# Small work beside the steps of two mixture-of-experts stages, cut into more pieces and placed at other steps

## The chip, the cores and the metric

The kernel runs on one core of a Trainium2 chip. A core has a matrix engine (TensorE, PE in the profile; its weight loads are PEld), a vector engine (VectorE, DVE), an activation engine (ScalarE, ACT), a general engine (GpSimd, POOL) and a queue that issues transfers (SyncE, SP). Each runs its own instruction list strictly in order, and they meet through semaphores. The metric is the device time of one execution in microseconds (us), lower is better; the median of three runs is given.

## The reference

The input is 2048 tokens of width 128. Four layers each hold an attention block and a feed-forward block, all in the same sandwich:

```python
x = x + _layernorm(_L2_ffn_ref(_layernorm(x, axis=-1), ...), axis=-1)   # 16 experts, top 4 of 2 groups, and a shared one
x = x + _layernorm(_L3_attn_ref(_layernorm(x, axis=-1), ...), axis=-1)  # linear attention
x = x + _layernorm(_L3_ffn_ref(_layernorm(x, axis=-1), ...), axis=-1)   # 8 experts, top 2
```

Only these last three of the eight blocks matter here. The first of them multiplies silu(gate) by up and takes it through down, for every expert and token, weighted by the routing. The attention takes q and k through elu(.) + 1, makes one product of keys and values over the 1024 tokens of a sequence (two chunks of the kernel), multiplies q by it and projects. The last block is softmax routing, gelu between two matrices per expert, and a weighted sum.

## The kernel before

Its stages are numbered by block: stage 5 is the 16-expert mixture, stage 6 the linear attention, stage 7 the 8-expert mixture. A stage handles the tokens in four chunks of 512 (c = 0 to 3), a chunk is four tiles of 128. Stage 5 has 25 steps per chunk (r), each one slice of hidden units; stage 7 has 32 (m). Stage 6 has no stretch of its own: it runs in pieces beside the steps of 5 and 7, as do the routing and everything between the blocks.

**A step of stage 5.** TensorE makes gate and up (three matmuls each, L1762 to L1764, since every operand is split into a rounded part and a rest) and, for the step three earlier, down (L1768, L1769, L1771; L1771 reads the rest). ScalarE makes silu of the gate (L1863), then copies the upper part of the last product (L1851). VectorE multiplies the gate by its weight (L1909), makes the rest of the last product (L1899) and then the product of gate and up (L1917). Down results gather in one bank, which ScalarE evicts (L1855) in step 2 of the next chunk.

**A step of stage 7.** TensorE: three matmuls for the hidden units, three for the step four earlier. ScalarE: gelu (L2174), copy (L2180), every fourth step an eviction. VectorE: the rest (L2249) and one of four stations of the weighted sum (L2225 to L2241). Its loops may be five steps apart at most (a ring of five buffers).

**Small work.** Functions named beside (pe_, act_ and dve_beside_moe5 and _moe7) say after which step of its main loop each engine does which small piece. Each engine counts its own steps, and an engine may be several steps ahead of another, so a piece in step 9 of TensorE and one in step 9 of VectorE don't run at the same time. The pieces:

- dve_y: statistics of a block's result (STY, MVY); GpSimd makes the scale of them. dve_x: adds the scaled result to the stream (L282), then makes statistics of the sum (L264, L267 into MVX). GpSimd (pool_x, L333 to L338) then normalises the rows into XN, pe_turn_x turns them (L397), act_turned copies them.
- lin_features, in part 0 and part 1 for each chunk: TensorE, ScalarE (exponential and relu, L1482 to L1494, with a table load before and one back to silu behind) and VectorE (L1502, L1507). lin_kv is TensorE's product of keys and values (L1514), which reads the features of two chunks; then lin_out and lin_proj.
- dve_route5_a to _d and dve_route7_a to _c: routing. In stage 7 ScalarE makes an exponential between a and b and one between b and c (L2060). turn_weights then turns the routing's weights (L2065), which a transfer spreads over the partitions later.

## Time and profile before

| | |
|---|---|
| median of 3 runs | 1632.12 us (1631.22 to 1632.94) |
| the profiled execution | 1629.69 us, its span 1627.9 us |
| TensorE's mean granted clock | 0.877 of full speed |
| busy over the span | PE 79%, DVE 66%, ACT 70%, POOL 17% |
| stage 5 | 1108 to 1382 us of the span |
| stage 7 | 1382 to 1628 us |

The profile is one execution. Its busy shares are means over eight blocks with different limits (the first two thirds are attention, where ScalarE's line L1035 alone is busy for 466 us), so the stretches of the two mixture stages are read apart. In a row, the number in square brackets at the end is how long the engine had been idle before the instruction, and what ended the idle time. Matmuls overlap, so a row's own duration is longer than the distance to the next.

### The profile page before, as it was taken

The numbers are of one execution on the slowest core, as the hardware profiler recorded it, in microseconds if no ns is written. First come the engines' busy times: TensorE is split into PE (matmuls) and PEld (weight loads), VectorE is DVE, ScalarE is ACT, GpSimd is POOL, SyncE is SP. The second block draws the span as 40 slices with busy tenths as digits, with TensorE's granted clock in tenths as the row PEclk, the third lists the DMA queues.
The fourth block names the chain that finished last, engine by engine and source line by source line (L and its number), as shares of the span: only waits on it lengthen the run. The fifth ranks groups of instructions, "written<-read, shape, count | busy, mean of one in ns | idle before, by whom it ended". The sixth has DMA issues, their size and how long they took to land.

```text
span 1627.9 us, 22138 instructions
## 1 busy us (share of the span) xinstructions
PE 1288.8 (79%) x8028; PEld 659.5 (41%) x8028; DVE 1079.5 (66%) x2031; ACT 1140.7 (70%) x1619; POOL 271.1 (17%) x361
## 2 busy tenths in 40 slices
PE   5598888876676777777777777678988988887996
PEld 2233333344011111111111144456767776665875
DVE  6877877054455664566456655556978679767898
ACT  3166777755999999999999834345555645876985
POOL 4500003042000000000000034083011034803000
PEclk9589999997688788878877899888999998999998
DMA  5611020002410000101000030002323225011111
GB/s 178 154 22 22 23 41 3 2 1 87 107 20 0 20 17 4 20 0 20 20 1 1 1 151 1 1 1 66 106 83 93 88 73 171 27 33 33 47 44 54
DMA packets 40765, 74.65 MB, mean 46 GB/s; under 512 B 6096, under 2 KB 10448, under 8 KB 39888
## 3 DMA queue, kind: packets, MB, share of 16 engines
q1 hardware_dynamic: 39792, 71.67, 15.6%
q10 hardware_dynamic: 864, 1.57, 0.3%
q8 instruction: 63, 1.03, 0.3%
q14 instruction: 46, 0.38, 0.1%
HBM read 59.26 MB, written 13.96 MB: 45 GB/s over the span
## 4 chain that ended last, share of the span: by engine, by line
PE 38%; ACT 24%; DVE 19%; issue 12%; POOL 4%; DMA 2%; SPq 0%; POOLq 0%; DVEq 0%; ACTq 0%
ACT SHARED L1035 15%; PE PS L823 4%; PE PS L992 4%; PE PS L979 3%; DVE NM L732 3%; DVE SHARED L1045 3%; PE PS L712 2%; PE PS L645 2%; PE PS L1762 2%; PE PS L787 2%; PE PS L1764 2%; PE PS L1763 2%; DVE KS L1917 2%; PE PS L1215 2%; PE PS L1771 2%
## 5 line engine op out<-in xcount | busy, mean ns | idle before, releaser
L1035 ACT ACTIVATE SHARED<-PS 128x1536 f32<-128x1536 f32 (+1 forms) x352 | 466.1, 1437 | 31.2 <-PE PS L979 30.2
L979 PE MATMUL PS<-QS,KS 51*128 51x512 bf16 (+1 forms) x1024 | 242.0, 461 | 134.1 <-ACT SHARED L1035 128.7
L1045 DVE TENSOR_TENSOR SHARED<-SHARED 128x1536 f32<-128x1536 f32 (+1 forms) x176 | 286.6, 1703 | 86.4 <-ACT SHARED L1035 86.4
L803 ACT ACTIVATE SHARED<-PS 128x512 f32<-128x512 f32 (+3 forms) x384 | 164.4, 494 | 96.6 <-PE PS L791 87.3
L979 PEld LDWEIGHTS PS<-QS,KS 51*128 51x128 bf16 (+1 forms) x1024 | 41.2, 99 | 386.8 <-ACT SHARED L1035 358.6
L992 PE MATMUL PS<-SHARED,Vg 128*16 128x512 f32 x1024 | 157.9, 694 | 1.7 <-DVE SHARED L1045 1.6
L732 DVE TENSOR_REDUCE NM<-PS 128x2 f32<-128x1024 f32 (+3 forms) x128 | 129.0, 1022 | 28.5 <-PE PS L718 20.4
L1762 PE MATMUL PS<-ROUNDED 128*128 128x512 f32 x328 | 138.8, 423 | 4.9 <-ACT KS L1863 4.2
L1763 PE MATMUL PS<-ROUNDED 128*128 128x512 f32 x328 | 132.5, 404 | 0.0
L1764 PE MATMUL PS<-ROUNDED 128*128 128x512 f32 x328 | 132.3, 403 | 0.0
L1851 ACT ACTIVATE ROUNDED<-KS 128x512 fp32r<-128x512 f32 x100 | 63.0, 630 | 82.8 <-DVE KS L1917 82.8
L1771 PE MATMUL PS<-ROUNDED 128*128 128x512 f32 x228 | 94.1, 413 | 22.3 <-DVE ROUNDED L2249 11.4
L476 POOL COPY Vg<-XH 128x256 f32<-128x256 f32 x16 | 6.3, 400 | 626.9 <-PE PS L992 396.9
L326 POOL TENSOR_SCALAR VEY<-MVY 128x4 f32<-128x4 f32 x32 | 8.4, 263 | 583.8 <-DVE MVY L267 582.6
L823 PE MATMUL PS<-SHARED,Vg 128*16 128x256 f32 (+3 forms) x1152 | 93.3, 397 | 11.2 <-ACT SHARED L803 9.6
L1768 PE MATMUL PS<-ROUNDED 128*128 128x512 f32 x228 | 92.1, 404 | 8.3 <-ACT ROUNDED L2180 3.7
L2249 DVE TENSOR_TENSOR ROUNDED<-KS,ROUNDED 128x512 fp32r<-128x512 f32 x103 | 75.1, 732 | 30.5 <-ACT ROUNDED L2180 29.7
L712 PE MATMUL PS<-SHARED 48*128 48x512 bf16 (+3 forms) x384 | 71.2, 370 | 29.9 <-DVE NM L732 18.4
L1769 PE MATMUL PS<-ROUNDED 128*128 128x512 f32 x228 | 91.2, 400 | 0.0
L2174 ACT ACTIVATE KS<-PS,C 128x512 f32<-128x512 f32 x103 | 71.1, 691 | 27.3 <-PE PS L1764 26.0
L1863 ACT ACTIVATE KS<-PS 128x512 f32<-128x512 f32 x100 | 58.8, 588 | 40.1 <-PE PS L1764 39.9
L1909 DVE TENSOR_TENSOR SHARED<-KS,SHARED 128x512 f32<-128x512 f32 x88 | 61.4, 698 | 35.3 <-ACT KS L1863 32.2
(265 smaller groups left out, 2314.4 us busy)
## 6 DMA issues: line engine op xcount, KB each, us to landing
SHARED<-wx SPq DMA_DIRECT2D x64, 256.0 KB, 3.1
qx<-SHARED SPq DMA_DIRECT2D x24, 256.0 KB, 4.0
SHARED<-in_moe SPq DMA_DIRECT2D x3, 1600.0 KB, 11.9
kx<-SHARED SPq DMA_DIRECT2D x18, 256.0 KB, 4.0
SHARED<-wx SPq DMA_DIRECT2D x16, 224.0 KB, 3.0
SHARED<-qx SPq DMA_DIRECT2D x16, 192.0 KB, 4.7
SHARED<-kx SPq DMA_DIRECT2D x16, 192.0 KB, 5.3
QS<-qx SPq DMA_DIRECT2D x16, 192.0 KB, 4.5
```

What stands on the lines that cost most here:

```text
L712: ins = pe.matmul(PS[:, slot(k, x):slot(k, x) + n], q[r, p, qt * P:qt * P + P], key[r, p, hi * CH:hi * CH + n], start=True, stop=not diag)
L732: dve.tensor_reduce(out=dst, in_=src, axis=AX.X, op=ALU.max, negate=True).then_inc(A[0, "a_red"], 1)
L803: act.activation(PB[t % 3][:, h, q0:CH], bank(RING0[n % 3], q0), ACT.Exp, scale=SCORE_SCALE)\
L823: ins = pe.matmul(PS[32 * h:32 * h + VC, 6 * CH + a:6 * CH + b], Vg[g % 2][:, kt, h, :], PB[t % 3][:, h, a:b], start=kt == 0, stop=last an ...
L979: ins = pe.matmul(bank((v % 2) * GRP + f - a), KS[g % 2][r, h // 2, kt * P:kt * P + P], QS[g % 2][r, h // 2, qh * CH:(qh + 1) * CH], start ...
L992: ins = pe.matmul(PS[32 * h:32 * h + VC, 6 * CH:7 * CH], Vg[g % 2][:, kt, h, :], EX[:, f * CH:f * CH + CH], start=kt == 0, stop=kt == KT - 1)
L1035: act.activation(dst, PS[:, (v % 2) * GRP * CH:((v % 2) * GRP + b - a) * CH], ACT.Exp if second == qh else ACT.Sigmoid, scale=SCORE_SCALE)\
L1045: dve.tensor_tensor(ex_tile(j), ex_tile(j), GR[w % RING][:, 0:(b - a) * CH], ALU.mult)\
L1762: pe.matmul(dst, w[0], x[0], start=start, stop=False)
L1763: pe.matmul(dst, w[0], x[1], start=False, stop=False)
L1764: return pe.matmul(dst, w[1], x[0], start=False, stop=stop)
L1771: return pe.matmul(dst, w[0], x[1], start=False, stop=stop)
```

## The change

The arithmetic stays. dve_x is cut in two, dve_x_sum (the addition) and dve_x_stats (the statistics), which may stand in different steps. Routing pieces are cut: b and c of stage 5 into b, b2 and c, c2; b of stage 7 into b and b2 (dve_top_k gives its second half to dve_top_k_ties). The two y pieces ahead of stage 7 get a step each. Where both halves are called in a row, nothing changes. The rest of the change is step numbers in the six tables:

| piece | before | after |
|---|---|---|
| stage 5, c 0: routing, VectorE | 4, 8, 12, 16 | 4, 7, 10, 13, 16, 19 |
| turned weights, TensorE / ScalarE | 20 / 21 | 22 / 23 |
| c 1, 2: x, VectorE | 6 | sum 7, statistics 8 |
| turning of x, TensorE / ScalarE | 9 / 10 | 11 / 12 |
| features part 0, TensorE / ScalarE / VectorE | 11 / 12 / 13 | 13 / 14 / 15 |
| features part 1, the same | 15 / 16 / 16 | 16 / 17 / 18 |
| c 2: kv, TensorE / VectorE | 18 / 18 | 19 / 20 |
| out, TensorE / ScalarE; proj | 20 / 21; 23 | 21 / 22; 24 |
| c 2, 3: y of the first two chunks for stage 7 | c 2: 24, 24 | c 3: 0, 1 |
| c 3: their x, VectorE | 0, 1 | sum 2, 3; statistics 3, 4 |
| their turning, TensorE / ScalarE | 4, 5 / 5, 6 | 6, 8 / 7, 8 |
| logits, TensorE; VectorE | 7, 8; 8 | 9, 10; 11 |
| y and x of chunk 2 for the attention, VectorE | 10, 12 | 13; sum 15, statistics 16 |
| its turning, TensorE / ScalarE | 17 / 18 | 19 / 20 |
| routing a, b, (b2,) c, VectorE | 9, 11, 13 | 12, 14, 17, 18 |
| its exponentials, ScalarE | 10, 12 | 13, 17 |
| turned weights, TensorE / ScalarE | 16 / 17 | 21 / 22 |
| stage 7, c 0: features (2, part 1), TensorE / ScalarE / VectorE | 9 / 10 / 11 | 8 / 9 / 11 |
| other attention pieces of c 0 | 10 to 27 | one step later; proj stays at 31 |
| c 1: y, y, VectorE | 1, 1 | 1, 2 |
| x, x, VectorE | 3, 5 | sum 4, 6; statistics 5, 7 |
| turnings, TensorE / ScalarE | 9, 10 / 10, 11 | 11, 13 / 12, 14 |
| logits, TensorE / VectorE | 14, 14 / 15, 15 | 16, 17 / 17, 18 |
| routing a, b, (b2,) c, VectorE | 16, 19, 24 | 19, 22, 24, 28 |
| its exponentials, ScalarE | 17, 22 | 20, 26 |
| turned weights, TensorE / ScalarE | 28 / 29 | 30 / 31 |
| c 2, 3: last x and shift, VectorE | 18, 22 | sum 18, 22; statistics and shift 19, 23 |

The lines of the diff that are more than a number, and of the numbers those of which the text speaks most:

```diff
@@ dve_x @@
         def dve_x(dve, own, e, c):
+            dve_x_sum(dve, own, e, c)
+            dve_x_stats(dve, own, e, c)
+
+        def dve_x_sum(dve, own, e, c):
             if e.norm_y:
...
                 ins.then_inc(x_sum, 1)
-                dve.wait_ge(x_sum, e.n_y(c))
...
+        def dve_x_stats(dve, own, e, c):
+            if e.norm_y:
+                dve.wait_ge(x_sum, e.n_y(c))
             if e.turn:
                 dve_stats(dve, own, STX, MVX, lambda t: tile(e.stream(), t), c).then_inc(x_var, 1)
...
-            own.link(dve.tensor_reduce(out=best[:, :, 7:8], in_=sel, axis=AX.X, op=ALU.add))
+            own.mark(dve.tensor_reduce(out=best[:, :, 7:8], in_=sel, axis=AX.X, op=ALU.add))
+
+        def dve_top_k_ties(dve, own, vals, e, k, sel, best, tmp, nt=NT):
+
+            a, b, c = tmp
+            own.wait()
...
@@ pe_beside_moe5 @@
             if c in (1, 2) and r == 16:
                 pe_lin_features(pe, c - 1, 1)
-            if c == 2 and r == 18:
+            if c == 2 and r == 19:
                 pe_lin_kv(pe, 0)
...
@@ dve_beside_moe5 @@
-            if c and r == (12 if c == 3 else 6):
-                dve_x(dve, own, edges[6], c - 1)
-            if c in (1, 2) and r == 13:
+            if c and r == (15 if c == 3 else 7):
+                dve_x_sum(dve, own, edges[6], c - 1)
+            if c and r == (16 if c == 3 else 8):
+                dve_x_stats(dve, own, edges[6], c - 1)
+            if c in (1, 2) and r == 15:
                 dve_lin_features(dve, c - 1, 0)
-            if c in (1, 2) and r == 16:
+            if c in (1, 2) and r == 18:
                 dve_lin_features(dve, c - 1, 1)
```

What this does to the order on an engine is shown at three places.

ScalarE in stage 5, chunk 2: what stands between the first burst of features (ends with L1494) and the second (begins with the load ahead of L1489), before. KS written by L1863 is the gate's silu, ROUNDED written by L1851 the copy.

```order
L1863 ACT_TABLE_LOAD
L1863 ACTIVATE KS<-PS 128x512
L1851 ACTIVATE ROUNDED<-KS 128x512
L1863 ACTIVATE KS<-PS 128x512
L1851 ACTIVATE ROUNDED<-KS 128x512
L1863 ACTIVATE KS<-PS 128x512
L1851 ACTIVATE ROUNDED<-KS 128x512
L1863 ACTIVATE KS<-PS 128x512
L1851 ACTIVATE ROUNDED<-KS 128x512
L1489 ACT_TABLE_LOAD
L1489 ACTIVATE Vg<-PS 128x256
L1490 ACTIVATE Vg<-PS 128x256
```

The same place after (L1863 is now L1882, L1851 L1870, L1489 L1496).

```order
L1882 ACT_TABLE_LOAD
L1882 ACTIVATE KS<-PS 128x512
L1870 ACTIVATE ROUNDED<-KS 128x512
L1882 ACTIVATE KS<-PS 128x512
L1870 ACTIVATE ROUNDED<-KS 128x512
L1882 ACTIVATE KS<-PS 128x512
L1870 ACTIVATE ROUNDED<-KS 128x512
L1496 ACT_TABLE_LOAD
L1496 ACTIVATE Vg<-PS 128x256
```

One silu and one copy fewer stand between the two bursts. VectorE's two features (L1502 and L1507) were and are three steps apart.

VectorE in stage 5, chunk 1: the x piece (L282, L264, L267) behind y (the first two rows), before.

```order
L264 BN_STATS STY<-PS 128x6 x4
L267 BN_AGGR MVY<-STY 128x2 x4
L1909 TENSOR_TENSOR SHARED<-KS,SHARED 128x512
L1899 TENSOR_TENSOR ROUNDED<-KS,ROUNDED 128x512
L1917 TENSOR_TENSOR KS<-SHARED,PS 128x512
L282 SCALAR_TENSOR_TENSOR X<-PS,RSY,X 128x128 x4
L264 BN_STATS STX<-X 128x6 x4
L267 BN_AGGR MVX<-STX 128x2 x4
L1909 TENSOR_TENSOR SHARED<-KS,SHARED 128x512
L1899 TENSOR_TENSOR ROUNDED<-KS,ROUNDED 128x512
```

And after (L282 is L286, L1909 L1928, L1899 L1918, L1917 L1936), from the step before the sum.

```order
L1928 TENSOR_TENSOR SHARED<-KS,SHARED 128x512
L1918 TENSOR_TENSOR ROUNDED<-KS,ROUNDED 128x512
L1936 TENSOR_TENSOR KS<-SHARED,PS 128x512
L286 SCALAR_TENSOR_TENSOR X<-PS,RSY,X 128x128 x4
L1928 TENSOR_TENSOR SHARED<-KS,SHARED 128x512
L1918 TENSOR_TENSOR ROUNDED<-KS,ROUNDED 128x512
L1936 TENSOR_TENSOR KS<-SHARED,PS 128x512
L264 BN_STATS STX<-X 128x6 x4
L267 BN_AGGR MVX<-STX 128x2 x4
L1928 TENSOR_TENSOR SHARED<-KS,SHARED 128x512
L1918 TENSOR_TENSOR ROUNDED<-KS,ROUNDED 128x512
L1936 TENSOR_TENSOR KS<-SHARED,PS 128x512
```

A step's three instructions now stand between sum and statistics, and one step more between y and the sum.

VectorE in stage 7, chunk 1: from the end of the second half of routing b (L2044) to the first instruction of c (L2049), before.

```order
L2044 TENSOR_TENSOR QS<-QS 128x64
L2249 TENSOR_TENSOR ROUNDED<-KS,ROUNDED 128x512
L2241 TENSOR_TENSOR SHARED<-SHARED 128x512
L2249 TENSOR_TENSOR ROUNDED<-KS,ROUNDED 128x512
L2225 TENSOR_SCALAR SHARED<-SHARED 128x512
L2249 TENSOR_TENSOR ROUNDED<-SHARED,ROUNDED 128x512
L2230 SCALAR_TENSOR_TENSOR SHARED<-SHARED 128x512
L2249 TENSOR_TENSOR ROUNDED<-KS,ROUNDED 128x512
L2238 TENSOR_TENSOR SHARED<-SHARED 128x512
L2249 TENSOR_TENSOR ROUNDED<-KS,ROUNDED 128x512
L2241 TENSOR_TENSOR SHARED<-SHARED 128x512
L2049 TENSOR_TENSOR QS<-QS 128x64
```

And after, from L2078 to L2083 (L2249 is now L2286).

```order
L2078 TENSOR_TENSOR QS<-QS 128x64
L2286 TENSOR_TENSOR ROUNDED<-KS,ROUNDED 128x512
L2262 TENSOR_SCALAR SHARED<-SHARED 128x512
L2286 TENSOR_TENSOR ROUNDED<-KS,ROUNDED 128x512
L2267 SCALAR_TENSOR_TENSOR SHARED<-SHARED 128x512
L2286 TENSOR_TENSOR ROUNDED<-SHARED,ROUNDED 128x512
L2275 TENSOR_TENSOR SHARED<-SHARED 128x512
L2286 TENSOR_TENSOR ROUNDED<-KS,ROUNDED 128x512
L2278 TENSOR_TENSOR SHARED<-SHARED 128x512
L2083 TENSOR_TENSOR QS<-QS 128x64
```

The end of b and the start of c were five steps apart and are four, while TensorE's turned weights moved by two steps and c by four.

## Rows read from the trace of the kernel before

**Rows 1.** Busy time by stretch (stages 5 and 7): us, then busy us per engine, granted clock

```profile
core 0: us, PE busy (x) PEld busy (x) DVE busy (x) ACT busy (x) POOL busy (x), PEclk, DMA share, GB/s
1108.00:1382.00 274.00, 243.76 (x1036) 192.47 (x1035) 219.79 (x477) 145.49 (x247) 52.49 (x60) 0.94 0.34 100
1382.00:1628.00 246.00, 208.52 (x884) 162.99 (x883) 193.72 (x413) 193.24 (x328) 57.23 (x64) 0.94 0.13 41
```

**Rows 2.** Timeline of VectorE, stage 5, start us, us, line, [idle before <-releaser]

```profile
1151.75 0.68 DVE L1917 TENSOR_TENSOR KS<-SHARED,PS 128x512 f32<-128x512 f32 x1
...
1153.13 0.69 DVE L1899 TENSOR_TENSOR ROUNDED<-KS,ROUNDED 128x512 fp32r<-128x512 f32 x1
1153.74 0.68 DVE L1917 TENSOR_TENSOR KS<-SHARED,PS 128x512 f32<-128x512 f32 x1
```

**Rows 3.** Timeline of VectorE and TensorE, stage 5, chunk 1, steps 6 to 9

```profile
1190.62 0.38 DVE L267 BATCH_NORM_AGGREGATE MVX<-STX 128x2 f32<-128x6 f32 x4
...
1192.23 0.51 PE L1771 MATMUL PS<-ROUNDED 128*128 128x512 f32 x1 [0.28 <-DVE ROUNDED L1899]
1196.61 1.12 PE L397 MATMUL PS<-ident,XN 128*128 128x128 f32 x4 [3.88 <-POOL XN L338]
```

**Rows 4.** Timeline of ScalarE, VectorE, TensorE, stage 5, chunk 2, steps 16 to 18

```profile
1286.39 1.28 ACT L1489 ACT_TABLE_LOAD   x1
...
1288.63 1.28 ACT L1863 ACT_TABLE_LOAD   x1
1289.93 0.60 ACT L1863 ACTIVATE KS<-PS 128x512 f32<-128x512 f32 x1
1290.42 0.62 ACT L1851 ACTIVATE ROUNDED<-KS 128x512 fp32r<-128x512 f32 x1
...
1288.37 0.42 DVE L1507 SCALAR_TENSOR_TENSOR XH<-Vg 128x256 f32<-128x256 f32 x1 [0.68 <-ACT Vg L1490]
...
1286.27 0.39 PE L1771 MATMUL PS<-ROUNDED 128*128 128x512 f32 x1
...
1288.31 0.39 PE L1771 MATMUL PS<-ROUNDED 128*128 128x512 f32 x1
1288.85 2.05 PE L1514 MATMUL PS<-QS,XH 128*128 128x128 f32 x16 [0.15 <-DVE XH L1507]
```

**Rows 5.** The same matmuls in stage 7 (timeline), and the stretch's busy times and clock

```profile
1434.95 3.61 PE L1514 MATMUL PS<-QS,XH 128*128 128x128 f32 x16 [2.11 <-DVE XH L1507]
...
1435.20:1438.60 3.40, 3.40 (x17) 3.40 (x17) 1.83 (x4) 0.22 (x1) 0.00 (x0) 0.50 0.03 10
```

**Rows 6.** Timeline of TensorE, stage 5, chunk 3, first half: both its waits

```profile
1316.96 0.47 PE L1768 MATMUL PS<-ROUNDED 128*128 128x512 f32 x1 [2.29 <-ACT SHARED L1855]
...
1324.85 0.66 PE L397 MATMUL PS<-ident,XN 128*128 128x128 f32 x4 [2.37 <-POOL XN L338]
```

**Rows 7.** Timeline of VectorE and TensorE, stage 5, chunk 3, steps 11 to 15

```profile
1344.82 0.21 DVE L2040 TENSOR_REDUCE QS<-QS 128x8 f32<-128x64 f32 x1
...
1348.84 0.23 DVE L2044 TENSOR_TENSOR QS<-QS 128x64 f32<-128x64 f32 x1
...
1350.33 0.79 PE L1771 MATMUL PS<-ROUNDED 128*128 128x512 f32 x1 [2.66 <-DVE ROUNDED L1899]
...
1354.90 0.63 PE L1771 MATMUL PS<-ROUNDED 128*128 128x512 f32 x1
```

**Rows 8.** Timeline of TensorE, stage 7, chunk 1: its waits in steps 8 to 10

```profile
1468.54 0.50 PE L1771 MATMUL PS<-ROUNDED 128*128 128x512 f32 x1 [1.59 <-DVE ROUNDED L2249]
...
1472.48 0.95 PE L397 MATMUL PS<-ident,XN 128*128 128x128 f32 x4 [2.06 <-POOL XN L338]
...
1478.24 0.66 PE L397 MATMUL PS<-ident,XN 128*128 128x128 f32 x4 [2.25 <-POOL XN L338]
```

**Rows 9.** Timeline of VectorE and TensorE, stage 7, chunk 1: last routing piece, turned weights

```profile
1512.70 0.29 DVE L2054 TENSOR_TENSOR SHARED<-QS 128x32 f32<-128x32 f32 x2
...
1510.20 0.43 PE L1771 MATMUL PS<-ROUNDED 128*128 128x512 f32 x1
...
1513.22 0.60 PE L2065 MATMUL PS<-ident,SHARED 128*16 128x128 f32 x4
```

More of the change, by code:

```diff
@@ L1698, in dve_route5_c, with dve_route5_c2 @@
                                    U5.rearrange("p t e -> p (t e)"), 0.0, ALU.mult, ALU.add)
[L1699 removed]
+            own.mark(dve.tensor_reduce(out=BEST5[:, :, 7:8], in_=SEL5, axis=AX.X, op=ALU.add))
+        def dve_route5_c2(dve, own, b):
+            own.wait()
             own.link(dve.tensor_scalar(BEST5[:, :, 7:8], BEST5[:, :, 7:8], -1.0, 4.0, ALU.mult, ALU.add))
@@ L1947, in dve_beside_moe5 @@
-            if c == 3 and r == 8:
+            if c == 3 and r == 2:
+                dve_x_sum(dve, own, edges[7], 0)
+            if c == 3 and r == 3:
+                dve_x_stats(dve, own, edges[7], 0)
+                dve_x_sum(dve, own, edges[7], 1)
+            if c == 3 and r == 4:
+                dve_x_stats(dve, own, edges[7], 1)
+            if c == 3 and r == 11:
                 dve_logits7(dve, 0)
                 dve_logits7(dve, 1)
-            if c == 3 and r == 9:
+            if c == 3 and r == 12:
@@ L1951, in dve_beside_moe5 @@
                 dve_route7_a(dve, own, 0)
-            if c == 3 and r == 11:
+            if c == 3 and r == 14:
                 dve_route7_b(dve, own, 0)
-            if c == 3 and r == 13:
+            if c == 3 and r == 17:
+                dve_route7_b2(dve, own, 0)
+            if c == 3 and r == 18:
                 dve_route7_c(dve, own, 0)
@@ L2289, in dve_beside_moe7 @@
             if c == 2 and m == 18:
-                dve_x(dve, own, edges["end"], 0)
+                dve_x_sum(dve, own, edges["end"], 0)
+            if c == 2 and m == 19:
+                dve_x_stats(dve, own, edges["end"], 0)
                 dve_shift(dve, own, 0)
@@ L2294, in dve_beside_moe7 @@
             if c == 2 and m == 22:
-                dve_x(dve, own, edges["end"], 1)
+                dve_x_sum(dve, own, edges["end"], 1)
+            if c == 2 and m == 23:
+                dve_x_stats(dve, own, edges["end"], 1)
                 dve_shift(dve, own, 1)
@@ L2299, in dve_beside_moe7 @@
             if c == 3 and m == 18:
-                dve_x(dve, own, edges["end"], 2)
+                dve_x_sum(dve, own, edges["end"], 2)
+            if c == 3 and m == 19:
+                dve_x_stats(dve, own, edges["end"], 2)
                 dve_shift(dve, own, 2)
```

140 lines of the change are left out of this document (78 added, 62 removed).

## The prediction, with its working

> **What bounds the kernel now.** The first view to read is the table of busy time by stretch [rows 1]. In stage 5 (the 16-expert mixture) TensorE is busy 243.76 of 274 us, in stage 7 (the 8-expert one) 208.52 of 246; VectorE and ScalarE have more slack in both. So the time of these stages is TensorE's work, plus the 30 and 37 us in which it stands, plus what a halved clock costs. A moved piece of small work counts only if it changes one of TensorE's waits. Hence the second view, the timelines around those waits, engine by engine.
>
> Two things are to be seen there. First, VectorE and ScalarE form a ring in stage 5: product L1917, ScalarE's rounded copy L1851, rest L1899, next product. A turn takes 1.99 us (1151.75 to 1153.74), and the rest and the product start 0.61 apart [rows 2]; the weighted gate L1909 is a third instruction of that kind, made while ScalarE copies. TensorE may be ahead of that ring by three steps, since its last matmul of step j reads the rest of step j-3. Work that VectorE does beside its steps delays the ring by about its own length, and TensorE stands only when the sum has eaten those three steps. Second, a wait for the bank that a turned tile, a feature or a product goes through can't be absorbed that way: TensorE's order is fixed and everything behind the waiting instruction stands.
>
> **Stage 5, chunk 0.** The routing of the second half is cut from four pieces into six. The instructions are the same; per piece the ring hides what of it falls into ScalarE's copy: a turn of 1.99 against three starts of 0.61 leaves 0.16 [rows 2]. Two more pieces hide 2 x 0.16 = 0.3 at most: **-0.3**, bounds -0.6 and 0.
>
> **Stage 5, chunks 1 and 2, the turned x.** Sum and statistics now stand a step apart, and the turning waits for the statistics: VectorE's statistics end at 1191.00, the normalised rows come out of GpSimd, and TensorE turns them at 1196.61, having stood 3.88 us [rows 3]. The chain of 5.6 us is untouched. Before, the statistics were in step 6 and the turning in step 9; now they are in 8 and 11, three steps again. The wait stays; what may go is the 0.28 that TensorE stood just ahead for the rest, since the same VectorE work is now spread over four steps and not two, and some 0.1 of covered time. **-0.4** for each chunk, -0.8 in all; bounds -4 (VectorE so well ahead that TensorE arrives later) and +0.5.
>
> **Stage 5, chunk 2, keys times values: the main term.** ScalarE's second burst of features holds a table load, three activations and the load back. It starts at 1286.39, the next gate L1863 starts at 1289.93 (3.54 later) and the copy behind it at 1290.42 (4.03 later). VectorE's features come at 1288.37, for they stood in the same step as the burst (16 and 16) and had only to wait for the activations; TensorE reached its matmuls L1514, three steps after the features' matmuls, at 1288.70 and stood 0.15 [rows 4]. In the new table TensorE is still three steps behind (16 and 19, where it was 15 and 18) and ScalarE still one behind TensorE (17), but VectorE's features move to step 18, one step behind the burst. Step 18's product has to be out before them; it needs the rest of step 17, which needs ScalarE's copy of step 17, which stands in ScalarE's order behind the load back and the gate of step 18. So: copy ends 4.03 + 0.63 = 4.66 after the burst's start, rest and product follow at 0.61 each [rows 2], the features start at about 4.74 + 1.22 = 5.96 and take 0.42, and the matmuls can start 6.44 after the burst's start. TensorE gets there, as before, 1288.70 - 1286.39 = 2.31 after it. It stands 4.1 us where it stood 0.15: **+4.0**. Bounds: +2.5 if TensorE reaches the spot later than it did, +5.5 if earlier. Nothing repays it: behind the matmuls TensorE has no further wait until 1316.96 [rows 6], so it is the bound of that stretch.
>
> Such waits also cost clock. The same matmuls in stage 7 came after a wait of 2.11 and took 3.61 instead of 2.05 us, and the clock granted in 1435.20 to 1438.60 was 0.50, the lower of its two levels (1.2 GHz) [rows 4, 5]. After a wait of 4 us I expect the same: 3.61 - 2.05 = **+1.6**; bounds 0 and +3.2 (the stretch twice as long).
>
> A rule against this reading of the burst: the row shows the load back taking 1.28, with the gate starting 1.30 after it began [rows 4]. The Trainium skill, "ScalarE: Activation LUTs", section "What ACT_TABLE_LOAD costs", puts a switch at 1.28 for the load and 1.38 more for a drain, 2.66 together. By the page the wait would be 1.4 longer and the sum +5.9 rather than the sum below; by the row it is not, and the row decides.
>
> **Stage 5, chunk 3.** First half: y, sum and statistics of the first two chunks of stage 7 were in steps 24, 0 and 1 and are now in 0 to 4. TensorE stood 2.29 for the release of the output bank and 2.37 for the second turned chunk [rows 6]. The eviction that releases the bank comes in step 2 of ScalarE, behind copies that waited for VectorE's pile of y and x; that pile now starts a step later and in smaller pieces, so I take the 2.29 as gone. The turnings stand in steps 6 and 8 behind statistics in 3 and 4: three steps for the first, where it was four, so by [rows 3] a wait returns there (VectorE's statistics of the second chunk queue behind it): 2.5, and 0.2 for the second. -2.29 - 2.37 + 2.7 = **-2.0**; bounds -4.7 and +1.5.
>
> Second half: routing b (L2040 at 1344.82 to L2044 at 1348.84, 4.2 us in one piece) and x behind it stop TensorE for 2.66, and a stretch at half clock follows [rows 7]: 2.7 of wait, and then 4.57 us for the step from 1350.33 to 1354.90 where a step takes 2.04 (1286.27 to 1288.31) [rows 4, 7]: 2.5 more. Now b, sum, statistics and b2 are in steps 14, 15, 16 and 17. Up to the statistics VectorE has y, the first half of b (2.1) and x beside its steps, where it had y and the whole of b (4.2) up to the wait of 2.66; x is about as long as the half that is gone, so I take 2.5 of waits to remain. But the turned x was five steps behind its statistics (12 and 17) and is now three (16 and 19), as in chunk 1, where that meant 3.88 [rows 3]: 3.9 more, and 1.6 for the clock behind it [rows 4, 5]. 2.5 + 3.9 + 1.6 - 2.7 - 2.5 = **+2.8**. The second half of the routing and ScalarE's exponential, now in one step (17), lie beside that wait. Bounds -1 (no wait at the turning) and +5.
>
> **Stage 7, chunk 1, the turned x.** Three waits: 1.59 for the rest behind x in one piece, 2.06 and 2.25 for the turned rows [rows 8]. The first goes with the split. The first turning stays six steps behind its statistics (3 and 9, now 5 and 11) and keeps its wait; the second goes from five to six (5 and 10, now 7 and 13) and gains a step of 1.36 us (six matmuls, where the nine of stage 5 take 2.04 [rows 4]): -1.59 - 1.36 = **-2.9**; bounds -6 (all three go) and 0.
>
> **Stage 7, chunk 1, the turned weights.** VectorE's last routing piece ended at 1512.99 and TensorE's turning followed at 1513.22 without a wait, 0.2 us to spare; the pieces were in steps 24 and 28 [rows 9]. They are now in 28 and 30, two steps apart and not four, and ScalarE's exponential, whose table loads put VectorE behind, moved by the same four steps (22 to 26). TensorE's end of step 26 was at 1510.20 + 0.23; the piece would be ready 2.5 after that. **+2.5**, and **+1.0** for the clock, rather over half of the 1.6 above since the wait is shorter; bounds for both 0 and +5. The routing cut in two there (steps 22 and 24 for 19) moves nothing: the exponential waits for b2 as it waited for b.
>
> **The rest of stage 7.** Of the 37 us in which TensorE stands there [rows 1], 5.9 are in the three waits above [rows 8]. In chunk 0 and at the end features and the last x move by a step or are split; a piece cut in two saved 1.59 where it alone held TensorE up. I take **-1.0** for all of this, less than one such wait; bounds -3 and +1.5.
>
> **Sum.** -0.3 - 0.8 + 4.0 + 1.6 - 2.0 + 2.8 - 2.9 + 2.5 + 1.0 - 1.0 = **+4.9**. The profiled execution took 1629.69 with a span of 1627.9, so the new span would be 1632.8. The median of the three runs is 1632.12, 2.4 above that execution, and the forecast is made on it: 1632.1 + 4.9 = **1637.0 us**, +0.3%.
>
> **The rivals.** *Less is lost than I say, and the result is no change.* The two terms at a turning (+2.8 in chunk 3) and at the weights (+3.5) rest on TensorE being at its full lead when it gets there. If VectorE's smaller pieces keep that lead short, these waits shrink: with half of each (-3.1) the time is 1633.9, with neither (-6.3) 1630.7. For it: the pieces are shorter everywhere. Against: the lead is set by sums of pieces, and they don't change.
>
> *Faster.* The halved clock follows TensorE's waits, and the change cuts the pieces behind five of them. If the waits of 2.66 in [rows 7] and all of [rows 8] go (-2.7 - 5.9) and with them two stretches at the lower clock (-2.5 - 1.6), this is -12.7; with +5.6 at keys times values, +3.5 at the weights and -4.1 for the remaining terms (-0.3 - 0.8 - 2.0 - 1.0) the sum is -7.7: 1624.4. With three quarters of the 12.7 it is -4.5: 1627.6. It decides at the turnings: if the waits L397 in chunks 1 to 3 fall below 1.5 us, it holds. Against: none of these turnings but one gets more steps behind its statistics.
>
> *Slower by more.* The waits feed one another: keys times values 5.5 with the clock down for longer, both half-clock stretches in chunk 3, weights 5: 1643.
>
> **How the numbers follow.** A measurement of this kernel can tell about 0.2% (3.3 us) from no change; the bounds are 1628.9 and 1635.4. Forecast case, 1635.4 to 1641: 0.44, with the chance of more, 0.05, within the slower ones. No change: 0.31. Faster: 0.20 in 1624 to 1628.9. The keys-times-values term is the surest, since it follows from the order alone; the gains in the same direction as the edit are counted only where a step is won. The range leaves out what lies under 1627 (0.10) and over 1641.5 (0.05): 1627 to 1641.5.
>
> **What would show it.** In the new profile: a wait of about 4 us of TensorE at the keys-times-values matmuls of stage 5, followed by matmuls of 0.6 us; waits of 3.5 to 4 at the turnings L397 of chunks 1, 2 and late in 3; the 2.29 behind the output bank gone; at the turned weights in stage 7 chunk 1 a wait of 2.5 where there was none. If the first is under 1 us, the argument on the ring is wrong, and with it the sign.

## The result, and the profile after

| | before | after |
|---|---|---|
| median, 8 runs each | 1631.67 us (1624.88 to 1636.97) | 1638.82 us (1637.49 to 1647.99) |
| ratio after to before | | 1.0055, 95% interval 1.0037 to 1.0074 |
| profiled execution, its span | 1629.69, 1627.9 us | 1638.77, 1637.0 us |
| mean granted clock of TensorE | 0.877 | 0.875 |

The change makes the kernel slower by 0.55%, 9 us by the ratio and 7.2 by the medians. The forecast was 1637.0 (+4.9 us) in a range of 1627.0 to 1641.5.

The stretches of the two stages first: us, busy us per engine (PE, PEld, DVE, ACT, POOL), granted clock. They answer [rows 1]; the third is the stretch behind the keys-times-values matmuls.

```profile
core 0: us, PE busy (x) PEld busy (x) DVE busy (x) ACT busy (x) POOL busy (x), PEclk, DMA share, GB/s
1108.00:1384.60 276.60, 243.52 (x1030) 190.90 (x1030) 217.14 (x470) 144.01 (x246) 52.53 (x62) 0.94 0.35 100
1384.60:1637.00 252.40, 213.66 (x883) 164.54 (x882) 191.34 (x413) 194.12 (x328) 57.22 (x62) 0.92 0.14 39
1291.85:1296.00 4.15, 4.15 (x18) 4.05 (x19) 1.75 (x3) 0.27 (x1) 0.00 (x0) 0.50 0.41 117
```

VectorE and ScalarE are hardly busier anywhere than before (ScalarE 194.12 for 193.24 in stage 7, the rest less). TensorE stands longer, and in stage 7 it is also busier at a lower clock. The line numbers have moved: L1781 to L1783 are the gate and up matmuls, L1787, L1788 and L1790 down, L404 the turning of x, L1521 keys times values, L2099 the turned weights; L1882 and L1870 are ScalarE's silu and copy, L1918 VectorE's rest in stage 5, L2286 the one in stage 7, L2216 ScalarE's copy there, L345 GpSimd's normalised rows, L2088 the last routing piece.

TensorE's timeline of the new kernel at the places that the prediction speaks of (in brackets the idle time ahead and what ended it):

```profile
1197.62 1.06 PE L404 MATMUL PS<-ident,XN 128*128 128x128 f32 x4 [3.62 <-POOL XN L345]
...
1263.37 1.12 PE L404 MATMUL PS<-ident,XN 128*128 128x128 f32 x4 [3.64 <-POOL XN L345]
...
1291.85 3.78 PE L1521 MATMUL PS<-QS,XH 128*128 128x128 f32 x16 [5.07 <-DVE XH L1514]
...
1326.34 0.66 PE L404 MATMUL PS<-ident,XN 128*128 128x128 f32 x4 [1.11 <-POOL XN L345]
1332.08 0.66 PE L404 MATMUL PS<-ident,XN 128*128 128x128 f32 x4 [0.98 <-POOL XN L345]
...
1362.59 1.12 PE L404 MATMUL PS<-ident,XN 128*128 128x128 f32 x4 [2.55 <-POOL XN L345]
1364.86 0.79 PE L1781 MATMUL PS<-ROUNDED 128*128 128x512 f32 x1 [1.15 <-ACT KS L1882]
...
1475.91 0.50 PE L1790 MATMUL PS<-ROUNDED 128*128 128x512 f32 x1 [0.43 <-DVE ROUNDED L2286]
1478.15 0.51 PE L1790 MATMUL PS<-ROUNDED 128*128 128x512 f32 x1 [0.58 <-DVE ROUNDED L2286]
1481.88 1.12 PE L404 MATMUL PS<-ident,XN 128*128 128x128 f32 x4 [3.23 <-POOL XN L345]
...
1515.73 0.51 PE L1790 MATMUL PS<-ROUNDED 128*128 128x512 f32 x1 [1.43 <-DVE ROUNDED L2286]
1517.94 0.50 PE L1787 MATMUL PS<-ROUNDED 128*128 128x512 f32 x1 [0.99 <-ACT ROUNDED L2216]
1522.99 1.02 PE L2099 MATMUL PS<-ident,SHARED 128*16 128x128 f32 x4 [3.83 <-DVE SHARED L2088]
```

Set beside the rows of before: the two turnings of [rows 3] keep their waits (3.62 and 3.64 for 3.88 each); keys times values stands 5.07 for 0.15 and takes 3.78 for 2.05 [rows 4]; the 2.29 of [rows 6] is gone; 2.66 in one wait [rows 7] became 2.55 and 1.15 at the turning and behind it; of the three waits of [rows 8] the second turning's is gone and the first's has grown; at the turned weights a wait of 3.83 stands where none was [rows 9].

To sum the times up, take the same matmul of the same step in both traces (the last of down, L1771 and L1790) and the difference of their start times. It is the lead or lag of the new kernel, and its change over a stretch is what that stretch cost. Where a small piece falls on different sides of a cut in the two kernels (the turned y, 0.4 us, and logits, 1.9), that is taken out of both sides.

| stretch | measured, us | forecast, us |
|---|---|---|
| ahead of stage 5 (the change isn't there) | -2.0 | 0 |
| stage 5, chunk 0 | -0.4 | -0.3 |
| chunks 1 and 2 up to the second burst | -1.8 | -0.8 |
| chunk 2, keys times values | +7.5 | +5.6 |
| chunk 3, first half | -3.9 | -2.0 |
| chunk 3, second half | +3.0 | +2.8 |
| stage 7, chunk 0 | +3.0 | part of -1.0 |
| chunk 1, turned x | -1.5 | -2.9 |
| chunk 1, routing and turned weights | +5.9 | +3.5 |
| chunks 2 and 3 | -0.7 | part of -1.0 |
| sum | +9.1 | +4.9 |

The first line is a difference between two executions and no effect of the change (e7 below, which has the kernel before's steps up to there, gets to stage 5 4.7 us earlier than that kernel's own profiled execution); the stages themselves lost 11.1 us.

### The profile page after: what moved, and what is told of

Same layout as the page of the kernel before. It is cut to its first block, busy times and chain, and to the rows that moved or that the text cites. A ratio compares the mean times of both kernels' runs of the same rounds, so it can differ in the third digit from the quotient of the medians.

```text
span 1637.0 us, 22138 instructions
## 1 busy us (share of the span) xinstructions
PE 1294.3 (79%) x8028; PEld 660.6 (40%) x8028; DVE 1076.7 (66%) x2031; ACT 1140.9 (70%) x1619; POOL 270.7 (17%) x361
## 4 chain that ended last, share of the span: by engine, by line
PE 37%; ACT 26%; DVE 20%; issue 13%; POOL 3%; DMA 1%; SPq 0%; ACTq 0%; DVEq 0%; POOLq 0%
ACT SHARED L1042 15%; PE PS L830 4%; PE PS L999 4%; PE PS L986 3%; DVE NM L739 3%; DVE KS L1936 2%; DVE SHARED L1052 2%; PE PS L719 2%; PE PS L652 2%; PE PS L794 2%; PE PS L1781 2%; PE PS L1783 2%; PE PS L1782 2%; PE PS L1222 2%; ACT SHARED L810 1%
## 5 line engine op out<-in xcount | busy, mean ns | idle before, releaser
L1781 PE MATMUL PS<-ROUNDED 128*128 128x512 f32 x328 | 138.3, 422 | 4.7 <-ACT KS L1882 4.0
L1783 PE MATMUL PS<-ROUNDED 128*128 128x512 f32 x328 | 132.4, 404 | 0.0
L1870 ACT ACTIVATE ROUNDED<-KS 128x512 fp32r<-128x512 f32 x100 | 63.0, 630 | 82.1 <-DVE KS L1936 82.0
L1790 PE MATMUL PS<-ROUNDED 128*128 128x512 f32 x228 | 94.9, 416 | 18.2 <-DVE ROUNDED L2286 9.4
L1787 PE MATMUL PS<-ROUNDED 128*128 128x512 f32 x228 | 92.5, 406 | 9.3 <-ACT ROUNDED L2216 5.6
L2286 DVE TENSOR_TENSOR ROUNDED<-KS,ROUNDED 128x512 fp32r<-128x512 f32 x103 | 75.1, 732 | 37.5 <-ACT ROUNDED L2216 36.7
L1788 PE MATMUL PS<-ROUNDED 128*128 128x512 f32 x228 | 91.0, 399 | 0.0
L1882 ACT ACTIVATE KS<-PS 128x512 f32<-128x512 f32 x100 | 58.8, 588 | 44.6 <-PE PS L1783 44.3
L1928 DVE TENSOR_TENSOR SHARED<-KS,SHARED 128x512 f32<-128x512 f32 x88 | 61.8, 702 | 41.2 <-ACT KS L1882 37.5
```

Of the source, the lines that this page charges most:

```text
L1781: pe.matmul(dst, w[0], x[0], start=start, stop=False)
L1783: return pe.matmul(dst, w[1], x[0], start=False, stop=stop)
L1790: return pe.matmul(dst, w[0], x[1], start=False, stop=stop)
```

## The experiments

Each kernel is the changed one with the edit shown, unless it says otherwise. Medians stand beside the changed kernel's 1638.8 us, which was not measured again in these sessions, and beside runs of the kernel before on the same chip in the same session (the ratios); the kernel before's own runs spread over some 12 us, so the readings rest on the traces, in differences of the same kind as in the table above.

**e1: VectorE's features back in the step of ScalarE's burst.**

```diff
-            if c in (1, 2) and r == 18:
+            if c in (1, 2) and r == 17:
                 dve_lin_features(dve, c - 1, 1)
```

> The changed kernel with one number back: VectorE's part 1 features in chunks 1 and 2 of stage 5 stand in step 17, the step of ScalarE's burst, and no longer in step 18. Theory (ring through ScalarE's load back): the wait of 5.07 us at the keys-times-values matmuls falls to under 1, the matmuls take about 2.1 and not 3.8 us, and the time is 6 to 8 us below the changed kernel's 1638.8: about 1632. Rival (VectorE is late there whatever its order, and what is won is waited for again at the output bank or the next turning): the wait falls by at most half, or the time stays within 2 us of 1638.8.

Measured: 1631.35 us, ratio to before 1.0006 (0.9985 to 1.0028). The timeline of TensorE:

```profile
1286.44 2.05 PE L1521 MATMUL PS<-QS,XH 128*128 128x128 f32 x16 [1.11 <-DVE XH L1514]
...
1294.27 1.98 PE L1534 MATMUL PS<-XH,QS 128*128 128x512 f32 x4 [1.66 <-DVE QS L1528]
```

The stretch costs 3.1 us over before and not 7.5, so one number of the table takes back 4.4 us at its place. The medians fall by 7.5, but the rest of that is not shown to be this edit's: the trace puts 1.3 us ahead of stage 5 and 2.2 in stage 7, where nothing was edited. The theory holds in the wait and in the clock; the wait that remains (1.11, not under 1) is because TensorE now comes nearly a microsecond earlier, below. Part of what was won is waited for again, as the rival has it, though at another place: the output's matmuls (L1534) stand 1.66 for VectorE's piece of keys times values (L1528), where they stood not at all before. The change moved that piece by two steps (18 to 20) and the output by one (20 to 21), and L1528 now starts 7.5 us after the keys-times-values matmuls, where it was 5.5. No run moves it back.

**e7: the kernel before with that number alone.**

```diff
-            if c in (1, 2) and r == 16:
+            if c in (1, 2) and r == 17:
                 dve_lin_features(dve, c - 1, 1)
```

> The kernel before with one number of the change: VectorE's part 1 features in chunks 1 and 2 of stage 5 in step 17 instead of 16, one step behind ScalarE's burst. Theory: the wait of 0.15 us at the keys-times-values matmuls becomes 4 to 5, the matmuls take 3.8 and not 2.05, and the time is 5 to 7.5 us over the kernel before, 1635.5 to 1638. Rival (the wait of the changed kernel needs the closer spacing of its two bursts as well): a wait of under 2 us, and under 3 us more in all.

Measured: 1639.71 us, ratio 1.0055 (1.0035 to 1.0075). TensorE:

```profile
1289.24 3.78 PE L1514 MATMUL PS<-QS,XH 128*128 128x128 f32 x16 [4.14 <-DVE XH L1507]
```

The wait of 4.14 is the one worked out in the prediction from the rows of before (4.1). From step 14 to step 22 of the chunk this kernel loses 6.2 us to the kernel before, and nothing of it is given back up to the end of stage 5. By the ratio the medians differ by 9 us, more than the 5 to 7.5 expected; the profiled execution, the fastest of the ten, shows the 6.2 and no more.

**e2: the turned weights of stage 7's chunk 1 later.**

```diff
-            if c == 1 and m == 30:
+            if c == 2 and m == 2:
                 pe_turn_weights7(pe, 1)
-            if c == 1 and m == 31:
+            if c == 2 and m == 3:
                 act_turn_weights7(act, 1)
```

> The changed kernel with the turning of the second half's weights (stage 7, chunk 1) four steps later: TensorE in step 2 of chunk 2 instead of step 30, ScalarE in step 3. Theory (TensorE arrives two steps too early): its wait of 3.83 us goes and nothing comes in its place, and the half-rate matmuls behind it go too: 5 to 6 us less than 1638.8, about 1633.5. Rival (VectorE is behind by the routing, and TensorE would wait for its rests instead): a wait for the rest of 2 to 4 us appears in steps 30 to 3, and the time falls by less than 2.5 us.

Measured: 1632.69 us, ratio 1.0019 (0.9992 to 1.0046). TensorE at the new place, and the waits of the routing ahead of it:

```profile
1516.60 0.50 PE L1790 MATMUL PS<-ROUNDED 128*128 128x512 f32 x1 [1.46 <-DVE ROUNDED L2286]
1518.80 0.50 PE L1787 MATMUL PS<-ROUNDED 128*128 128x512 f32 x1 [1.01 <-ACT ROUNDED L2216]
...
1526.81 0.60 PE L2099 MATMUL PS<-ident,SHARED 128*16 128x128 f32 x4
```

The 3.83 are gone, nothing takes their place, and the stretch from step 24 to the next chunk costs 5.2 us less. The theory holds.

**e6: e2 with the second exponential and the last routing piece later.**

```diff
-            if c == 1 and m == 26:
+            if c == 1 and m == 28:
                 act_route7(act, 1, 1)
-            if c == 1 and m == 28:
+            if c == 1 and m == 29:
                 dve_route7_c(dve, own, 1)
```

> e2 (weights turned in steps 2 and 3 of chunk 2) with the second exponential of stage 7's chunk 1 in ScalarE's step 28 instead of 26 and the last routing piece in VectorE's 29 instead of 28. In e2 TensorE stood 0.98, 1.46 and 1.01 us there, then half rate. If ScalarE's wait for the piece b2 is what holds the gelus up, these three waits fall to under 1.5 us in sum, and the time is 2 to 4 us under e2's 1632.7. If the two table loads of 2.6 us themselves are more than the lead, the waits only move two steps: the time stays within 1.5 us of e2's.

Measured: 1630.19 us, ratio 1.0013 (0.9994 to 1.0032). The waits ahead of the exponential stay (0.98 and 1.43: those are VectorE's b and b2), the 1.01 behind it for ScalarE's copy goes, and with it the matmuls at half rate: over 1495.0 to 1528.7 the granted clock is 1.00, where in the changed kernel over the like stretch it is 0.92. It took 3.1 us more off the trace than e2 (whose clock there is 0.95), with one wait of 1.01 gone. The first theory is right in its direction and wrong in its sum: the waits sum up to 2.4 and not under 1.5, and two thirds of the gain is clock.

**e3: the turning of x in chunk 3 later.**

```diff
-            if c and r == (19 if c == 3 else 11):
+            if c and r == (22 if c == 3 else 11):
                 pe_turn_x(pe, edges[6], c - 1)
```

(ScalarE's part from 20 to 23.)

> The changed kernel with the turning of chunk 2's x in chunk 3 of stage 5 three steps later: TensorE 22 for 19, ScalarE 23 for 20. Theory (three steps between statistics and turning are too few, six are enough): the wait of 2.55 us goes and with it the 1.15 behind it and the half-rate stretch: 4 to 5 us less than 1638.8, about 1634. Rival (the routing's b2 with the exponential in the same step holds TensorE up there anyway, and the turning only lay over it): a wait for the rest of 2 to 3 us in its place, and the time within 1.5 us of 1638.8.

Measured: 1637.14 us, ratio 1.0055 (1.0028 to 1.0082). TensorE:

```profile
1357.78 0.50 PE L1790 MATMUL PS<-ROUNDED 128*128 128x512 f32 x1 [0.64 <-DVE ROUNDED L1918]
1363.10 0.80 PE L1781 MATMUL PS<-ROUNDED 128*128 128x512 f32 x1 [4.82 <-ACT KS L1882]
```

The theory falls: the turning's wait went and one of 4.82 for silu took its place. The rival holds in the time (the stretch takes 50.3 us, as in the changed kernel), but not in the wait that it named, one for the rest. The timeline of ScalarE in the changed kernel shows what lay under the turning:

```profile
1357.14 0.63 ACT L1870 ACTIVATE ROUNDED<-KS 128x512 fp32r<-128x512 f32 x1 [1.72 <-DVE KS L1936]
1357.79 1.28 ACT L2094 ACT_TABLE_LOAD   x1
1362.64 0.26 ACT L2094 ACTIVATE QS<-QS 128x64 f32<-128x64 f32 x1 [3.56 <-DVE QS L2078]
1362.91 1.28 ACT L1882 ACT_TABLE_LOAD   x1
1364.21 0.60 ACT L1882 ACTIVATE KS<-PS 128x512 f32<-128x512 f32 x1
```

ScalarE loads the exponential's table, stands 3.56 for VectorE's b2, and all its silus stand behind that.

**e5: the exponential later as well.**

```diff
-            if c == 3 and r == 17:
+            if c == 3 and r == 19:
                 act_route7(act, 0, 1)
-            if c == 3 and r == 18:
+            if c == 3 and r == 20:
                 dve_route7_c(dve, own, 0)
```

(Turning of x in 21 and 22, turned weights in 23 and 24.)

> The changed kernel with the end of chunk 3 of stage 5 spread: turning of x in TensorE's step 21 and ScalarE's 22 (19, 20), ScalarE's second exponential in step 19 (17), VectorE's last routing piece in 20 (18), the turned weights in 23 and 24 (21, 22). In e3 the wait at the turning went and one of 4.82 us behind the exponential's load back took its place. Theory (the exponential stands in ScalarE's order only one step behind the piece it waits for, and keeps the next gate's silu behind it): with three steps between, both waits go, from step 13 of chunk 3 to the start of stage 7 about 4 us less than in the changed kernel, about 1635. Rival (VectorE is that late whatever stands behind it; the waits are its sum of work): waits for the rest of 3 us or more in their place and the time within 1.5 us of 1638.8.

Measured: 1639.35 us, ratio 1.0058 (1.0039 to 1.0077). Both waits went, but waits of 1.99 and 2.17 for VectorE's rests came, and the stretch takes 52.2 us, 1.9 more than in the changed kernel. The theory falls. In sum TensorE stands no longer than there (10.3 us in both); what is added is 2.0 us of busy time, for matmuls of 0.63 us follow behind each of the two new waits, where the changed kernel has one such stretch there. VectorE is the late one at both. The second wait, at 1373.24, lies in VectorE's slow stretch near the end of the stage, shown below; the first, at 1362.19, is ahead of it.

**e9: the second half of chunk 3 in whole pieces again.** b and b2 both in VectorE's step 14, exponential in ScalarE's 15, sum and statistics both in 15, the last piece in 16, turned weights in 19 and 20, turning of x in 20 and 21.

> The changed kernel with the second half of chunk 3 of stage 5 as in the kernel before, three steps later: routing b and b2 together in VectorE's step 14, the exponential in ScalarE's 15, x in one piece in 15, the last piece in 16, turned weights in 19, turning of x in 20 (five steps behind the statistics, as before). The stretch from the tenth step to the start of stage 7 took 46.9 us before and 50.3 in the changed kernel, 50.3 with the turning moved away alone and 52.2 with the exponential moved away too. If the cut and the spacing cost it: 47 us, time 3 to 4 us under 1638.8. If it is the three steps by which everything there is later (it comes closer to the end of the stage, where VectorE's instructions run slower beside GpSimd): 50 us or more and the time within 1.5 us of 1638.8.

Measured: 1636.35 us, ratio 1.0048 (1.0028 to 1.0068). The stretch takes 47.7 us and not 50.3, against 46.9 before. TensorE:

```profile
1355.53 0.49 PE L1790 MATMUL PS<-ROUNDED 128*128 128x512 f32 x1 [2.68 <-DVE ROUNDED L1918]
1356.53 0.50 PE L1781 MATMUL PS<-ROUNDED 128*128 128x512 f32 x1 [0.50 <-ACT KS L1882]
```

One wait of 2.68, as the 2.66 before, is less than the cut pieces cost: over the stretch TensorE stands 7.6 us, before 7.3, in the changed kernel 10.3. Cutting made no less work for VectorE, and it pulled statistics and turning together and b2 and the exponential too. Which of the two distances costs how much e3 and e5 don't separate. That it is the cut and the spacing, and not the three steps by which everything there is later, this run shows: those are worth the 0.8 that is left.

**e4: chunk 0 of stage 7 as before.** The table's steps for features, turning, keys times values and output of the kernel before.

> The changed kernel with the steps of stage 7's chunk 0 as in the kernel before (features, turning, keys times values and output pieces one step earlier, the first of them one step later). In the trace of the changed kernel TensorE lost 3.0 us more than before over that chunk. If the placement makes that loss: 3 us less, about 1636, with the waits of chunk 0 as in the kernel before. Rival (it is how the stage is entered, after a later chunk 3, that makes the loss): the chunk takes the same as in the changed kernel, 1638.8.

Measured: 1634.93 us, ratio 1.0041 (1.0014 to 1.0069). The chunk takes 71.9 us, where it took 74.0 in the changed kernel and 71.0 before: 2.1 of the 3.0 are the placement. (Over all the traces the chunk takes 72.8 to 74.0 with the steps of the change and 70.9 to 71.9 with those of before.) The same chunk before, after and in e4 (columns as in the first table of this kind):

```profile
1390.30:1461.30 71.00, 60.95 (x258) 45.92 (x259) 49.82 (x68) 58.30 (x100) 31.64 (x31) 0.98 0.07 23
1392.70:1466.70 74.00, 64.54 (x258) 47.36 (x259) 48.01 (x68) 58.41 (x99) 31.33 (x30) 0.93 0.07 22
1391.50:1463.40 71.90, 62.14 (x259) 46.80 (x260) 49.79 (x68) 58.27 (x99) 31.66 (x31) 0.95 0.07 23
```

TensorE stands 10.1, 9.5 and 9.8 us of it: the loss is none of waiting in sum but of the clock, granted at 0.98, 0.93 and 0.95. ScalarE's burst for features (2, part 1) was the one piece that moved a step earlier. VectorE's timeline there in the changed kernel:

```profile
1404.08 2.49 DVE L2286 TENSOR_TENSOR ROUNDED<-KS,ROUNDED 128x512 fp32r<-128x512 f32 x2 [0.23 <-ACT ROUNDED L2216]
1413.12 0.69 DVE L2286 TENSOR_TENSOR ROUNDED<-SHARED,ROUNDED 128x512 fp32r<-128x512 f32 x1 [2.44 <-ACT ROUNDED L2216]
```

It stands 2.44 for the first copy behind the burst, and TensorE right after it (1.19, behind a wait of 1.63). Over 1412.4 to 1424.0 the clock is then 0.85, where it was 1.00 in the like stretch before. e4 puts all pieces of the chunk back at once, so that it is this burst and not another piece is argued from these rows, not shown by a run.

**e10: the turning of x in chunk 1 of stage 5 later.**

```diff
-            if c and r == (19 if c == 3 else 11):
+            if c and r == (0, 13, 11, 19)[c]:
                 pe_turn_x(pe, edges[6], c - 1)
```

(ScalarE's part in 14; the features of that chunk two steps later on all three engines.)

> The changed kernel with chunk 1 of stage 5 alone altered: x turned in TensorE's step 13 and ScalarE's 14 (11, 12), and the features two steps later too. Theory (a turning three steps behind the statistics stands for GpSimd's chain of 5.6 us, one of five steps doesn't): the wait of 3.62 us goes, the half-rate matmuls behind it too; chunk 1 is 5 us shorter, time about 1634. Rival (the lead is then eaten elsewhere, by the bursts of features): 2 us or less.

Measured: 1631.88 us, ratio 1.0018 (0.9998 to 1.0038). TensorE:

```profile
1196.71 0.60 PE L404 MATMUL PS<-ident,XN 128*128 128x128 f32 x4
...
1201.80 1.12 PE L1473 MATMUL PS<-SHARED,W 128*128 128x512 f32 x2 [0.39 <-ACT SHARED L380]
```

The turning goes without a wait, and up to step 4 of the next chunk the trace is 4.6 us shorter than in the changed kernel: 3.6 of wait less the 0.39 behind it, and 1.3 because a wait of 1.39 for the output bank at the start of chunk 2, which the change had brought with it (none before), is gone too. The clock gives nothing: it is 0.97 over chunk 1 in both, for the wait of 2.85 for silu, later in the chunk, is now the one with the slow matmuls behind it. The expectation was right in the wait and wrong in where the rest comes from. Another 1.3 us came later in chunk 2, where nothing was edited. The wait was in the kernel before too; it was there to be had, and the change, which moved the turning by two steps, moved the statistics by two as well.

**e8, e11, e12: the repairs together.** e8 is e1, e2 and e4. e11 is e1, e4, e6, e9 and e10. e12 is e11 with the turning of chunk 2 in step 12 instead of 11 and what follows it in that chunk one step later.

> The changed kernel with e1, e2 and e4 together: features of VectorE in step 17, weights turned in chunk 2, chunk 0 of stage 7 as before. If the three losses are separate, as theory has it (4.4, 5.5 and 2.2 us in the traces), the time is 1638.8 - 12 = about 1627, 3 to 5 us under the kernel before. If what one repairs another has paid for already, 1630 to 1632.

> The changed kernel with what held in the runs before put together: chunk 1's turning and features two steps later (e10), VectorE's part 1 features in the step of ScalarE's burst (e1), routing and x of chunk 3 in whole pieces (e9), chunk 0 of stage 7 as before (e4), turned weights and second exponential of stage 7 later (e6). If the losses lie at separate waits, their savings in the traces add: 4.7 + 4.4 + 2.6 + 2.2 + 8 = 22 us under 1638.8, about 1617, some 13 us under the kernel before (ratio 0.992). If the slack that one uses is what another needs, 1624 (as e8) or above.

> e11 with the turning of chunk 2 of stage 5 one step later (12 for 11) and all that follows in that chunk. By the distance a step takes 2.04 us off the wait of 3.6 there: 2 us under e11, more if the half-rate matmuls go too. Rival: the output and projection of the attention now come at the end of the chunk, and stage 7's y waits for them: no gain over e11.

| | median, us | ratio to before (95%) |
|---|---|---|
| e8 | 1624.59 | 0.9967 (0.9946 to 0.9989) |
| e11 | 1616.62 | 0.9923 (0.9891 to 0.9955) |
| e12 | 1611.56 | 0.9879 (0.9851 to 0.9907) |

The savings add: 12 us were expected for e8 and 14.2 measured, 22 us were summed from the single runs for e11, and 1638.8 - 1616.6 = 22.2 were measured. e12 gained 5.1 more in the medians where 2 were expected. Its profiled execution is only 1.6 below e11's, but it came to stage 5 2.1 later; from there on its trace is 3.7 shorter, nearly all of it in chunk 2. So the step is worth more than the 2, and the 5.1 is not shown. In e12's trace the waits in chunk 2 are these, for 3.64 and 5.07 in the changed kernel, and the 1.66 at the output that e1 has as well:

```profile
1262.19 0.66 PE L404 MATMUL PS<-ident,XN 128*128 128x128 f32 x4 [1.59 <-POOL XN L345]
1283.89 2.05 PE L1521 MATMUL PS<-QS,XH 128*128 128x128 f32 x16 [1.09 <-DVE XH L1514]
...
1291.72 1.98 PE L1534 MATMUL PS<-XH,QS 128*128 128x512 f32 x4 [1.66 <-DVE QS L1528]
```

e12 beats the kernel before by 1.2% and the changed one by 27 us, with the same instructions.

## Why the prediction was right, point by point

The main term and the direction are right by mechanism. That the median came within 2 us of the forecast is in part luck: six of the eight terms are off by 1 us or more, to both sides.

**Keys times values: right in mechanism and place, 1.9 too small.** The chain from the burst's start was put at 5.96 us to VectorE's features. Timelines of ScalarE and VectorE in the changed kernel:

```profile
1285.40 1.28 ACT L1496 ACT_TABLE_LOAD   x1
...
1288.94 0.60 ACT L1882 ACTIVATE KS<-PS 128x512 f32<-128x512 f32 x1
1289.43 0.62 ACT L1870 ACTIVATE ROUNDED<-KS 128x512 fp32r<-128x512 f32 x1
...
1290.17 0.68 DVE L1918 TENSOR_TENSOR ROUNDED<-KS,ROUNDED 128x512 fp32r<-128x512 f32 x1
1290.78 0.68 DVE L1936 TENSOR_TENSOR KS<-SHARED,PS 128x512 f32<-128x512 f32 x1
1291.37 0.42 DVE L1514 SCALAR_TENSOR_TENSOR XH<-Vg 128x256 f32<-128x256 f32 x1
```

1291.37 - 1285.40 = 5.97. The first thing that was off is TensorE's arrival: 1291.85 - 5.07 = 1286.78 is 1.38 after the burst's start, not the 2.31 of the kernel before. In e7, where the two bursts keep their spacing of four steps, the wait was the 4.1 of the working; with three steps between, 5.07. That was the upper bound's case (+5.5), and it makes 0.9 of the 1.9. The other 1.0 is clock: the matmuls themselves cost 1.7 (3.78 for 2.05), as forecast, but the gate's matmuls behind them ran at clock 0.50 too, about 0.8 more, 2.6 for the 1.6 of the term. The load back took 1.28 with silu 1.30 behind its start here too, so the trace goes on disagreeing with the drain of 1.38 that the Trainium skill, "ScalarE: Activation LUTs", section "What ACT_TABLE_LOAD costs", adds. The sum that the prediction names for that case, +5.9, is a slip: 4.9 and 1.4 make +6.3.

**Turnings three steps behind their statistics: right.** 3.62 and 3.64 in chunks 1 and 2, forecast to stay at 3.9; e10 shows what they cost. The gain there was 1.8 for both chunks, the term 0.8. In chunk 3 the gain was 3.9 for 2.0. The first half's waits were 1.11 and 0.98 and not 2.5 and 0.2; with one of 0.21 ahead of them that is 2.4 us less waiting than before, for the 2.0 of the term, so the wait that returns was sized nearly right in sum. The other 1.5 was left out: behind the second turning the kernel before ran at clock 0.51 over 1325.9 to 1329.3, and in the changed kernel the clock is 1.00 over the whole first half.

**Chunk 3, second half: right sum (+3.0 for +2.8), partly by luck.** The turning's wait was 2.55 and not 3.9, but 1.15 behind it for the silu after the exponential had been counted as covered. e3 shows that it wasn't: with the turning away the exponential alone costs 4.82. The sentence that b2 and the exponential "lie beside that wait" is the step that failed; they were an equal limit below it. The term's parts missed in opposite ways: it had 3.7 more of waiting and 0.9 less of slow clock, and measured were 3.0 more of waiting (10.3 us for 7.3) and no change of the clock (0.86 for 0.85).

**Stage 7, chunk 0: wrong sign.** -1.0 was put on all that was left of stage 7, by analogy with a split piece; the chunk lost 3.0, and e4 gives 2.1 of it to the placement. No piece there was split. The failed step is the analogy, which counts waits: they are 0.6 us less in sum, and the clock (0.93 for 0.98) took more than they gave. The rows to price it, the burst's hole for VectorE and what follows, weren't among those read for that term, and its bound (+1.5) was too low.

**Stage 7, chunk 1: x -1.5 for -2.9, weights and routing +5.9 for +3.5.** The wait at the second turning went, as said, but all of it; TensorE, no longer held at 1468.54 [rows 8], came to the first turning earlier and stood 3.23 there for 2.06. Of the 1.59 for the rest, counted as gone, 0.43 and 0.58 remain. A gain ahead of a fixed chain is partly stood off at its end, and that was left out. At the turned weights the wait was 3.83 for 2.5, and by e2 the place cost 5.2 where 3.5 was forecast. That leaves 0.7 for the routing, whose cut was to move nothing: in waits that was right (before 0.69 and 3.30, after 0.53, 0.96, 1.43 and 0.99). The clock over the changed kernel's stretch 1492.2 to 1534.1 is 0.92, over the like stretch before (1490.2 to 1524.3) and in e2 it is 0.95, and of the 2.1 us by which TensorE's work took longer than before, 1.4 go with the weights' wait, whose clock term was 1.0. The 3.1 us that e6 takes off beyond e2 lead 2.4 below the kernel before: they were there to be had, and the change had not brought them.

**The rivals.** "No change" needed the waits at the turning and at the weights to shrink: neither did by half. "Faster" was to be decided by the turnings falling under 1.5: they did in the first half of chunk 3 alone. The sum of the terms, +4.9, lies 4 to 6 us under what the traces lost (9.1 in all, 11.1 in the stages) and 2 under the medians' 7.2; that it is no further off is due to errors of both signs in it.

## What to carry to other kernels

As far as these runs of one kernel go: when small work is placed beside the steps of several engines, the quantity to keep is the distance in steps between a piece and what waits for it, less the lead that the engines have over one another; a piece that waits for another engine's burst belongs in the burst's own step, for one step further it has that engine's next main work ahead of it as well. Cutting pieces brought little by itself (0.4 us in chunk 0 of stage 5, where little else was changed). If the cut pushes its end closer to a fixed chain behind it (statistics, GpSimd, turning), the chain's reader has to move by as much. And a place is priced by its waits and its clock together: chunk 0 of stage 7 lost 3 us with less waiting than before.
